# Grouped convolution and quantised dense layer: conv columns ordered block first, rounding shared by bank

## What is computed

```python
# x [64, 64, 1024], weight [64, 16, 9] (4 groups), kernel [1024, 1024], all fp32
h = conv1d(x, weight, padding=4, groups=4)                    # over the length of 1024
h = h + (cond @ c_weight.T)[:, :, None] + bias[None, :, None]
xq = fake_quant(h, bits=8, axis=-1)       # absmax over a row of 1024, round to whole levels
kq = fake_quant(ffn_kernel, bits=8, axis=0)
y  = xq @ kq + fake_quant(ffn_bias, bits=16, axis=-1)
out = x + fake_quant(y, bits=8, axis=-1)
```

## Time and profile before

| | us |
|---|---|
| median of 3 runs | 280.97 |
| lowest, highest | 279.25, 282.17 |
| the profiled execution | 278.56 |
| its span, first to last instruction | 276.7 |

### The profile page before, as it was taken

The page is one execution under the profiler, slowest core; times in us unless marked ns, Lnnn a source line. Parts: engine busy times, 40 slices in busy tenths (PEclk is TensorE's granted clock), DMA queues, the critical chain, the costliest instruction groups (busy, mean ns, idle before and its releaser), DMA issues.

```text
span 276.7 us, 4240 instructions
## 1 busy us (share of the span) xinstructions
PE 251.1 (91%) x1372; PEld 163.5 (59%) x1372; DVE 238.8 (86%) x509; ACT 185.2 (67%) x278; POOL 153.8 (56%) x71
## 2 busy tenths in 40 slices
PE   7866769999999999999999999999999999997540
PEld 3555557666666666666666666666666666663210
DVE  1799964799999999999999999999999989999984
ACT  6257586477777777777777777777777767564762
POOL 2533333356666666666666666666666666533453
PEclk9979999999999999999999999999999999999996
DMA  6997322406666565566666766666666663333355
GB/s 253 416 408 301 123 84 103 153 0 227 223 203 212 211 202 212 203 217 217 209 204 210 230 228 228 228 227 226 219 203 197 218 218 117 144 142 139 107 220 219
DMA packets 15799, 56.04 MB, mean 203 GB/s; under 512 B 1954, under 2 KB 1954, under 8 KB 15778
## 3 DMA queue, kind: packets, MB, share of 16 engines
q1 hardware_dynamic: 15488, 55.71, 56.8%
q10 hardware_dynamic: 290, 0.07, 0.1%
HBM read 38.99 MB, written 16.78 MB: 202 GB/s over the span
## 4 chain that ended last, share of the span: by engine, by line
PE 81%; DVE 8%; ACT 4%; DMA 3%; issue 2%; SPq 0%; DVEq 0%
PE dense_ps L427 36%; PE conv_ps L396 31%; PE turn_ps L416 5%; PE conv_ps L386 5%; DMA k_raw<-ffn_kernel 3%; DVE dense_ps L550 2%; DVE y L559 2%; DVE y_max L604 2%; ACT kq L279 2%; PE small_ps L407 2%; PE dense_ps L449 1%; DVE k_max L523 1%; ACT a_int L304 1%; PE dense_ps L440 1%; ACT x_hi L265 1%
## 5 line engine op out<-in xcount | busy, mean ns | idle before, releaser
L427 PE MATMUL dense_ps<-kq,a_t 128*128 128x512 bf16 x512 | 120.6, 379 | 6.1 <-DVE y L559 5.0
L218 POOL TENSOR_TENSOR x_lo<-xwin,x_hi 128x1032 fp32r<-128x1032 f32 x32 | 76.6, 2393 | 80.8 <-ACT x_hi L265 80.8
L227 POOL TENSOR_TENSOR o_sb<-y,o_sb 128x1024 f32<-128x1024 f32 x31 | 73.9, 2384 | 32.8 <-ACT y L315 32.7
L427 PEld LDWEIGHTS dense_ps<-kq,a_t 128*128 128x128 bf16 x512 | 48.9, 101 | 53.7 <-issue 6.7
L295 ACT CAST a_t<-turn_ps 128x1024 bf16<-128x1024 int16 x32 | 32.4, 1012 | 48.5 <-PE turn_ps L416 48.5
L564 DVE TENSOR_REDUCE small_ps<-conv_ps 128x8 f32<-128x1024 f32 x32 | 39.4, 1232 | 13.8 <-PE conv_ps L396 13.5
L550 DVE SCALAR_TENSOR_TENSOR dense_ps<-dense_ps,row_scale,k_scale_b 128x512 f32<-128x512 f32 x64 | 47.7, 745 | 3.6 <-PE dense_ps L427 3.6
L312 ACT ACTIVATE y_int<-y,y_inv 128x1024 int16<-128x1024 f32 x31 | 35.6, 1148 | 22.3 <-DVE y_inv L611 22.1
L559 DVE TENSOR_TENSOR y<-dense_ps,bq 128x512 f32<-128x512 f32 x64 | 43.9, 685 | 2.8 <-ACT bq L288 1.6
L604 DVE TENSOR_REDUCE y_max<-y 128x1 f32<-128x1024 f32 x32 | 38.7, 1210 | 0.7 <-issue 0.2
L304 ACT ACTIVATE a_int<-conv_ps,inv 128x128 int16<-128x128 f32 x128 | 36.0, 363 | 1.1 <-DVE inv L590 1.1
(11 more groups left out here) (55 smaller groups left out, 160.2 us busy)
## 6 DMA issues: line engine op xcount, KB each, us to landing
xwin<-x_windows SPq DMA_DIRECT2D x32, 516.0 KB, 4.8
o_sb<-x_rows SPq DMA_DIRECT2D x32, 512.0 KB, 5.3
out<-o_sb SPq DMA_DIRECT2D x31, 512.0 KB, 2.9
k_raw<-ffn_kernel SPq DMA_DIRECT2D x4, 1024.0 KB, 10.5
w_raw<-taps SPq DMA_DIRECT2D x2, 256.0 KB, 3.2
b_row<-ffn_bias SPq DMA_DIRECT2D x1, 512.0 KB, 15.9
out<-o_sb SPq DMA_DIRECT2D x2, 256.0 KB, 2.7
condt<-cond_t ACTq DMA_DIRECT2D x1, 32.0 KB
```

The lines of the kernel that those rows point to most:

```text
L218: pool.tensor_tensor(x_lo[:, at].rearrange("p n b -> p (n b)"), xwin[:, t % XWIN, :], x_hi[:, at].bitcast(F32).rearrange("p n b -> p (n b) ...
L227: pool.tensor_tensor(o_sb[:, at, :], y[:, t % YRING, :], o_sb[:, at, :], ALU.add).then_inc(s["o_made"], 1)
L427: mm = pe.matmul(dense_ps[:, h, :], a_t[:, t % LEVELS, q].rearrange("b j o -> b (j o)"), kq[:, q, half(h)], start=(q == 0), stop=(q == Q - 1))
```

## The change

The columns of the conv result are ordered block first, sample second: column = block x 8 + sample. Bank 0 then holds blocks 0 to 63 of all 8 samples and bank 1 blocks 64 to 127. The windows come from the host in the order [129 blocks, 8 samples], so the moving operand of every L396 matmul is one run of 512 elements, which starts at (64 hs + ch) x 8. The moving operand of the L386 matmuls is now the 8 columns of `select`, side by side, repeated 64 times. What leaves the PSUM for `a_int` keeps its order there (sample, block), so its readers walk the bank in steps of 8 elements: column_max over both banks, VectorE's rounding over the first 64 blocks of all samples in one instruction, ScalarE's rounding over the last 64 blocks in eight instructions of 64 columns where there were four of 128. Sizes, semaphores, the loops and the amount of data moved stay.

```diff
-        x_hi = sb("x_hi", [P, XSPLIT, NS, WIN], F32R)
-        x_lo = sb("x_lo", [P, XSPLIT, NS, WIN], F32R)
+        x_hi = sb("x_hi", [P, XSPLIT, WIN * NS], F32R)
+        x_lo = sb("x_lo", [P, XSPLIT, WIN * NS], F32R)
-        def conv_cols(at):
-            return conv_ps[:, at].rearrange("p h (n b) -> p (h n) b", b=BLOCKS)
+        def conv_half(at, h):
+            return conv_ps[:, at, h, :].rearrange("p (b n) -> p n b", n=NS)
+
+        def a_half(at, h):
+            return a_int[:, at].rearrange("p (n h b) -> p h n b", h=2, b=BH)[:, h]
 # round_levels (ScalarE)
-                for n in range(NS // 2, NS):
-                    ins = act.activation(a_int[:, at, n * BLOCKS:(n + 1) * BLOCKS],
-                                         conv_cols(at)[:, n, :], ACT.Copy,
-                                         scale=inv8[:, at, n:n + 1])
+                for n in range(NS):
+                    ins = act.activation(a_half(at, 1)[:, n, :], conv_half(at, 1)[:, n, :],
+                                         ACT.Copy, scale=inv8[:, at, n:n + 1])
 # conv (TensorE)
-                    ns = slice(n0 + hs * NH, n0 + (hs + 1) * NH)
                     mm = pe.matmul(
-                        conv_ps[:, at, hs, :].rearrange("p (n b) -> p n b", n=NH),
+                        conv_ps[:, at, hs, :].rearrange("p (b n) -> p b n", n=NS),
                         ctx2[:, g].rearrange("k q o -> k (q o)"),
-                        select[:, ns].unsqueeze(2).to_broadcast([P, NH, BLOCKS]),
+                        select[:, n0:n0 + NS].unsqueeze(1).to_broadcast([P, BH, NS]),
                         start=True, stop=False, skip_group_check=True)
...
+                            c0 = (hs * BH + ch) * NS
                             mm = pe.matmul(
-                                conv_ps[:, at, hs, :].rearrange("p (n b) -> p n b", n=NH),
+                                conv_ps[:, at, hs, :],
                                 w[:, ch, g].rearrange("p q o -> p (q o)"),
-                                x[:, x_at, hs * NH:(hs + 1) * NH, ch:ch + BLOCKS],
+                                x[:, x_at, c0:c0 + HALF],
                                 start=False, stop=False, skip_group_check=True)
 # column_max (VectorE)
-                                  conv_ps[:, t % 2].rearrange("p h (n b) -> p (h n) b", b=BLOCKS),
+                                  conv_ps[:, t % 2].rearrange("p h (b n) -> p n (h b)", n=NS),
 # levels (VectorE)
-                dve.tensor_tensor(a_int[:, at, 0:HALF].rearrange("p (n b) -> p n b", b=BLOCKS),
-                                  conv_cols(at)[:, 0:half_n, :],
-                                  inv8[:, at, 0:half_n].unsqueeze(2)
-                                  .to_broadcast([P, half_n, BLOCKS]), ALU.mult
+                dve.tensor_tensor(a_half(at, 0), conv_half(at, 0),
+                                  inv8[:, at].unsqueeze(2).to_broadcast([P, NS, BH]), ALU.mult
                                   ).then_inc(s["a_rounded_dve"], 1)
 # kernel (host): the windows' last two axes change places
-    windows = padded.reshape(N // NS, NS, GROUPS, CG, WIN, Q)[..., ::-1].transpose(0, 2, 5, 3, 1, 4)
+    windows = padded.reshape(N // NS, NS, GROUPS, CG, WIN, Q)[..., ::-1].transpose(0, 2, 5, 3, 4, 1)
```

More of the change, by code:

```diff
@@ L25 @@
 HALF = 512
-NH = HALF // BLOCKS
+BH = BLOCKS // 2
 JH = HALF // P
@@ L217, in split @@
                 at = t % XSPLIT
-                pool.tensor_tensor(x_lo[:, at].rearrange("p n b -> p (n b)"),
-                                   xwin[:, t % XWIN, :],
-                                   x_hi[:, at].bitcast(F32).rearrange("p n b -> p (n b)"),
+                pool.tensor_tensor(x_lo[:, at], xwin[:, t % XWIN, :], x_hi[:, at].bitcast(F32),
                                    ALU.subtract).then_inc(s["lo_made"], 1)
@@ L264, in round_x @@
                 wait(act, "lo_made", t - XSPLIT + 1)
-                act.copy(x_hi[:, t % XSPLIT].rearrange("p n b -> p (n b)"),
-                         xwin[:, t % XWIN, :]).then_inc(s["hi_made"], 1)
+                act.copy(x_hi[:, t % XSPLIT], xwin[:, t % XWIN, :]).then_inc(s["hi_made"], 1)
             def k_round(fb):
@@ L592, in levels @@
                 wait(dve, "a_turned", t - 1)
-                half_n = NS // 2
-                dve.tensor_tensor(a_int[:, at, 0:HALF].rearrange("p (n b) -> p n b", b=BLOCKS),
-                                  conv_cols(at)[:, 0:half_n, :],
-                                  inv8[:, at, 0:half_n].unsqueeze(2)
-                                  .to_broadcast([P, half_n, BLOCKS]), ALU.mult
+                dve.tensor_tensor(a_half(at, 0), conv_half(at, 0),
+                                  inv8[:, at].unsqueeze(2).to_broadcast([P, NS, BH]), ALU.mult
                                   ).then_inc(s["a_rounded_dve"], 1)
@@ L659 @@
     arrays = {
-        "x_windows": windows.reshape(TILES, P, NS * WIN),
+        "x_windows": windows.reshape(TILES, P, WIN * NS),
         "x_rows": x.transpose(0, 2, 1, 3, 4).reshape(TILES, P, L),
```

## The result

The changed kernel takes 283.28 us (median of 6 runs, 282.71 to 284.16) against 281.0 us before: a ratio of 1.0098, 95% interval 1.0052 to 1.0144. It is slower by 2.3 us. The forecast was 277.1 us, with 27 steady tiles faster by 4.5 us in all.

The account below looks back on a forecast made before the run. TensorE's stream was taken to bound steady tiles at 7.333 us, with VectorE next. 27 tiles at 7.165 us gain 4.5, the first turn costs 0.6: -3.9 from 280.97 gives 277.1 us, range 273.5 to 285.5.

Parts of the forecast that it names:

- Change 1: TensorE's conv matmuls (L396): one run of 512 takes 216 ns instead of 235, saving 0.225 us per tile.
- first rival: Conv matmuls stay at 235 ns because fp32 is read no faster; only the first turn is later, 281.6 us; chance 0.28.
- Change 2: TensorE's conditioning matmuls (L386): eight elements repeated 64 times still take 215 ns each.
- second rival: Run breaks cost, 0.28 us more per conditioning matmul (L386), 0.56 per tile; 290.8 us; chance 0.12.
- Change 3: ScalarE's rounding in eight instructions takes 1.72 us, 0.59 more; bounds +0.4 to +1.07 us.
- Change 4: VectorE's column_max and rounding read the PSUM in steps of eight; no added time taken.
- The sum: Steady tiles gain 4.5 us, the first turn loses 0.6, the end nothing: -3.9 us, giving 277.1 us.
- The loop that I worked out: Steady tiles: column_max, ScalarE's rounding, turn and TensorE's round take 14.33 us per two periods, so 7.165 us each.
- Dear ScalarE instructions: ScalarE's small rounding instructions cost 1.07 us more; 284.0 us with faster conv, 287.1 with slow conv; chance 0.08.
- The range: Total time from 273.5 to 285.5 us, leaving out the two slow rivals, 0.20.

Follow-up runs that it names:

- rates: Kernel before, followed by rows of 24 fp32r matmuls per form of moving operand, all else idle at first; one run took 227 ns, four runs 233 ns.
- act8_before: Kernel before with only ScalarE's rounding cut into eight instructions of 64 columns; 284.23 us, ratio to before 1.0113.
- act8_first4: Kernel before with ScalarE's rounding in eight pieces for tiles 0 to 3 alone; 283.92 us, ratio 1.0113.
- fill_before: Kernel before with unread bf16 matmuls in two TensorE waits, 6 ahead of the first turn and 9 in k=3; 279.23 us, ratio 0.9937.
- act8_rest: Kernel before with ScalarE's rounding in eight pieces for tiles 4 to 31 alone; 281.89 us, ratio 1.0032.
- act4_after: Changed kernel with ScalarE's rounding in four instructions of 128 columns, every second sample's own scale left out; 280.65 us, ratio to before 0.9984.
- fill_first_after: Changed kernel with 8 unread bf16 matmuls ahead of the first turn alone; 281.5 us, ratio 1.0031.
- fill_more_before: Kernel before with unread bf16 matmuls in all places where TensorE waits in the start; 279.22 us, ratio 0.9946.

## Why the prediction was wrong, point by point

**Change 1, the conv matmuls (the first step that failed).** The bounds were 216 and 235 ns, and I chose 216, since "an excess of only 9% looks more like a few hiccups than like a rate". The excess stays with one run: 227 ns at best, 232 in the mix of starts here, so 12 x 3 ns = 0.04 us per tile came instead of 0.225. The first rival had named this and its plain reason (4 bytes per column against 2). The row that I used against the fp32 path, the conditioning matmuls at 215 ns, was weak evidence: `rates` shows that an operand that repeats its data doesn't feel the limit.

**Change 2.** Right: 0.44 us for two matmuls, and the second rival is out; 60 more run breaks cost at most 4 ns per matmul, not 280.

**Change 3, the rounding (the second step that failed).** The length was right (1.72 forecast, 1.73 measured), and the busy time didn't matter in steady tiles. What failed is where it shows: I counted +0.6 us at the first turn and nothing after it, "these tiles wait for the quantised kernel". That wait is itself released by ScalarE, behind the rounding: another +0.61. And I priced waits of TensorE at their length, where in this trace each cost another 1.6 us of half clock.

**Change 4.** Right: nothing. The Trainium skill, Advanced Engine Details and Errata, section Memory Cachelines, wants consecutive elements together in the PSUM; VectorE's 1233 and 691 ns do not show it.

**The sum, steady part.** Forecast -4.5 us, measured -0.57 between tiles 4 and 31. The loop that I worked out never bound, as TensorE stayed the longer one. Of 27 x 0.03 = 0.8 us, 0.28 went once, at tile 28: ScalarE's round came 0.3 us later there in both kernels, which 0.73 us of slack absorbed before and 0.10 did not (the turn at 235.96, with the 0.13 of issue in the chain above ahead of it).

**The base.** The profile before was not typical. Over 92 runs of the kernel before, taken beside these experiments, the mean granted clock falls in three groups: 0.984 and up, 31 runs, median 279.1 us; 0.975 to 0.981, 20 runs, 281.0; up to 0.974, 41 runs, 281.9. The profiled execution (0.986) is of the first; all six runs of the changed kernel have 0.969 to 0.974. So against the trace that I read the change costs 4.5 us, against the median 2.3, and against runs of a like clock (0.972 to 0.974, four of the changed kernel, median 283.1) 283.1 - 281.9 = 1.2 us. The rounding's two waits less the steady gain are 2 x 0.61 - 0.57 = 0.65 us. With fillers the change costs just that, 279.85 - 279.23 = 0.6. The rest of the 2.3 us, some 1.6, is the clock's by difference, and the runs speak for it: all 18 runs of the three kernels whose first tiles round in eight pieces without fillers (the changed kernel, `act8_before`, `act8_first4`) lie at 0.975 or lower, where fewer than half of the kernel before's do (41 of 92). Why the clock falls in one execution and not in the next is open. That the profile lay 2.4 us under the median stood in the table, and I did not ask why.

**The rivals and the range.** The first rival (281.6) had the mechanism of the steady part right and missed the start. Dear ScalarE instructions were right in direction and wrong in kind: the instructions were as cheap as expected. The range held the time by luck: 283.28 lies near the 284.0 of the dear instructions, which did not come, and the time went up where it was forecast to fall by 3.9 us.

## What to carry to other kernels

Work added to an engine that is 67% busy is not free where the pipeline fills: look at each wait of the bound engine in the first tiles, who releases it, and what stands ahead of the releaser in its queue. A longer wait of TensorE costs its length and perhaps the clock of what follows, so compare the granted clock of several runs before taking one trace as the base, and try filling such waits: two places with 15 idle matmuls made this kernel 0.6% faster (`fill_before`, 279.2 us), faster than both kernels of this case. Don't take 216 ns for an fp32r matmul of 512 columns with fresh data: here it was 227 to 237 with one run.

## What the runs showed of the hardware

- A 512-column fp32r matmul at full clock takes 218 ns where the moving operand repeats eight elements or one, 227 to 234 with one fresh run from an even element (227 to 229 where it starts at a multiple of 64 bytes of `x_hi`), 237 from an odd element, 233 to 235 with four runs and 240 with eight. At 1.2 GHz the four runs take 427 ns, no more than 512 columns need.
- GpSimd, ScalarE, VectorE and loads beside it move this by less than 1 ns (loads were tried on one run alone).
- Reads of the PSUM in steps of eight fp32 are free for VectorE. ScalarE's instructions of 64 start 0.20 us apart, those of 128 0.256 us apart.
- TensorE's clock fell to 1.2 GHz behind waits of 2.25 and 2.86 us in the changed kernel, and stayed at 2.4 behind waits of 1.64 and 2.21 us in the trace before; in other traces it went otherwise: it fell behind 2.21 us in `act8_rest` and 2.25 in `act4_after`, and stayed behind 2.85 in `fill_first_after`. Around the wait of 1.4 to 1.6 us for tile 1's `x_hi` (1.63 before, ahead of the earlier trace rows) it fell in every trace but that of `fill_more_before`, where fillers stood in it. The length of the last wait alone does not decide.
